# Loading and splitting three weight matrices on GpSimd inside the last four batches of cross attention

## The reference

```python
# x: 32 x 100 x 256, ctx: 32 x 361 x 256; heads 16 of 16
x = x + tanh(g_xattn) * cross_attention(layernorm(x), ctx, mask)   # 32 batches, Wq, Wk, Wv, Wo: 256 x 256
xn = layernorm(x)
gate_v, gate_o = top2_gates(sigmoid(xn @ sel_v.T)), top2_gates(sigmoid(xn @ sel_o.T))  # sel: 64 x 256 each
q, k = xn @ q_w.T, xn @ k_w.T             # q_w, k_w: 1024 x 256, 8 heads of 128
v = sum_e gate_v[e] * (xn @ v_w[e])       # 8 experts a head
ctx = softmax(q @ k.T * SCALE) @ v
x = x + tanh(g_ffn) * sum_e gate_o[e] * (ctx @ o_w[e])
```

## Time and profile before

| | us |
|---|---|
| median of 3 runs | 1932.93 |
| lowest and highest run | 1931.02, 1933.18 |
| span of the profiled execution | 1928.9 |
| PE busy in it | 1873.3 (97%) |
| DVE, ACT, POOL busy in it | 1496.2, 1135.1, 935.0 |

### The profile page before, as it was taken

How to read it: one execution, slowest core, us unless ns; L and a number is a source line. 1 busy time by engine, 2 the same in 40 slices (tenths; PEclk the granted TensorE clock), 3 DMA queues, 4 the chain that set the end, 5 groups by cost and what they waited for, 6 DMA issues and landing times. The chain is left out here.

```text
span 1928.9 us, 57544 instructions
## 1 busy us (share of the span) xinstructions
PE 1873.3 (97%) x13454; PEld 1146.6 (59%) x13454; DVE 1496.2 (78%) x4309; ACT 1135.1 (59%) x3591; POOL 935.0 (48%) x1368
## 2 busy tenths in 40 slices
PE   6899999999997999999999999999999999999998
PEld 3688888888875555444444445545555555555543
DVE  6788888888887962555555556658999999999989
ACT  3688888888885444444444445445555555555543
POOL 4022222222212012666666666666677676776767
PEclk9999999999998999999999999999999999999999
DMA  6678887888752484000000022122222222222201
GB/s 156 127 116 119 118 120 118 120 120 118 119 87 93 205 330 181 27 27 27 14 27 27 27 85 94 52 64 71 71 80 67 79 75 71 79 69 77 75 13 66
DMA packets 192148, 174.22 MB, mean 90 GB/s; under 512 B 51921, under 2 KB 183378, under 8 KB 190034
## 3 DMA queue, kind: packets, MB, share of 16 engines
q1 hardware_dynamic: 189906, 165.06, 37.9%
q0 software_dynamic: 2176, 8.39, 1.3%
HBM read 112.41 MB, written 60.98 MB: 90 GB/s over the span
## 5 line engine op out<-in xcount | busy, mean ns | idle before, releaser
L1489 POOL TENSOR_TENSOR o_side<-o_side,o_tmp 128x256 f32 (+1 forms) x528 | 396.2, 750 | 196.6 <-POOL o_side L1489 70.5
L1258 PE MATMUL e_pv<-e_vw,e_xhi 128*128 (+1 forms) x1600 | 475.9, 379 | 1.2 <-ACT e_out L1181 1.2
L1191 ACT ACTIVATE big<-e_pv,gates 128x128 f32<-128x128 f32 x800 | 228.6, 369 | 280.1 <-PE e_pv L1258 278.5
L654 ACT ACTIVATE c_ex<-c_sm,c_nmax 100x361 f32<-100x361 f32 x512 | 302.7, 593 | 58.0 <-DVE c_nmax L537 49.5
L1617 ACT ACTIVATE o_tmp<-o_py,gates 128x256 f32<-128x256 f32 x528 | 222.3, 475 | 194.1 <-PE o_py L1689 123.3
L1689 PE MATMUL o_py<-o_whi,a_chi 128*128 128x512 f16 x800 | 304.9, 381 | 0.1
L1689 PE MATMUL o_py<-o_wlo,a_chi 128*128 128x512 f16 x800 | 304.5, 381 | 0.0
L1689 PE MATMUL o_py<-o_whi,a_clo 128*128 128x512 f16 x800 | 304.3, 380 | 0.0
L1258 PE MATMUL e_pv<-e_vw,e_xlo 128*128 (+1 forms) x800 | 303.2, 379 | 0.0
L537 DVE CUSTOM_DVE_ANT_0 c_sm<-c_ps,c_mbias 100x361 f32<-100x361 f32 x512 | 269.0, 527 | 38.4 <-PE c_ps L739 32.6
L1124 DVE TENSOR_SCALAR e_acc<-e_pv,gates 128x128 f32<-128x128 f32 x400 | 121.8, 346 | 225.9 <-PE e_pv L1258 225.8
(11 more groups left out here) (164 smaller groups left out, 3213.4 us busy)
## 6 DMA issues: line engine op xcount, KB each, us to landing
qk<-e_out SPq DMA_DIRECT2D x16, 1600.0 KB, 5.2
c_kst<-k_parts SPq DMA_DIRECT2D x256, 90.2 KB, 4.9
a_q<-qk SPq DMA_DIRECT2D x64, 200.0 KB, 2.4
a_k<-qk SPq DMA_DIRECT2D x64, 200.0 KB, 2.4
v<-e_out SPq DMA_DIRECT2D x20, 640.0 KB, 3.3
a_v<-v SPq DMA_DIRECT2D x64, 200.0 KB
c_ctx<-in_ctx_t SPq DMA_DIRECT2D x32, 361.0 KB, 3.5
e_wst<-in_v_w POOLq DMA_DIRECT2D x8, 1024.0 KB, 7.6
```

The source lines that it names most:

```text
L654: act.activation(ex[:, h % 4, 0:SK], sm[:, h % 4, :], ACT.Exp, scale=-1.0, bias=nmax[:, h % 4:h % 4 + 1], accum_out=den[:, b.par, HEAD[h]: ...
L1191: act.activation(tmp[:, hh, e, :], p_v[:, hh, 1, e * PD:(e + 1) * PD], ACT.Copy, scale=gate).then_inc(s_av, 1)
L1258: last = pe.matmul(p_v[:, hh, half, :], a[:, c, bass.ds(t * P, P)], vw[:, bass.ds(col + (w * DC + c) * VW, 512)], start=j == 0, stop=j == ...
L1489: pool.tensor_tensor(side[:, x.t, :], side[:, x.t, :], tmp[:, slot(x, r), j, :], ALU.add).then_inc(s_pool, 1)
```

## The change

The buffers of the three matrices (e_wst, e_qkhi, e_qklo, e_sst, e_shi, e_slo) are allocated before the first block, beside cross attention's own. SP starts the three loads at the end of its `body(28)`. POOL waits for all three at the end of its own `body(28)`, splits the selector there, and then two of the eight parts of the query and key weights (a part is 128 x 2 x 256 elements) at the end of each of `body(28)` to `body(31)`. In the second block the loads, ACT's and DVE's copies for the three matrices and the waits for them are gone; PE waits for the ninth low part instead, and projects queries and keys in one loop.

```diff
+            def load_router():
+                sp.dma_start(f.sst[:, :, :], sel_t.rearrange("(c p) e -> p c e", p=P)).then_inc(f.s_loaded, 16)
+                for w, src in enumerate((q_t, k_t)):
+                    sp.dma_start(f.wst[:, w, :, :], src.rearrange("(c p) n -> p c n", p=P)
+                                 ).then_inc(f.s_loaded, 16)
+
+            def body_and_router(b):
+                body(b)
+                if isinstance(b.n, int) and b.n == NB - 4:
+                    load_router()
...
-                batches(sp, body)
+                batches(sp, body_and_router)
...
+            def split_selector():
+                pool.wait_ge(f.s_loaded, 48)
+                pool.tensor_scalar(f.shi[:, :, :], f.sst[:, :, :], WS, None, ALU.mult).then_inc(f.s_high, 1)
+                pool.wait_ge(f.s_high, 1)
+                pool.tensor_scalar(f.sst[:, :, :], f.sst[:, :, :], WS, None, ALU.mult).then_inc(f.s_scaled, 1)
+                pool.wait_ge(f.s_scaled, 1)
+                pool.tensor_tensor(f.slo[:, :, :], f.sst[:, :, :], f.shi[:, :, :],
+                                   ALU.subtract).then_inc(f.s_low, 1)
+
+            def split_router(n):
+
+                w, part = divmod(n, PARTS)
+                src = f.wst[:, w, :, part * PART:(part + 1) * PART]
+                cut = slice(w * H * PD + part * PART, w * H * PD + (part + 1) * PART)
+                pool.wait_ge(f.s_loaded, 48)
+                pool.tensor_scalar(f.qkhi[:, :, cut], src, WS, None, ALU.mult).then_inc(f.s_high, 1)
+                pool.wait_ge(f.s_high, n + 2)
+                pool.tensor_scalar(src, src, WS, None, ALU.mult).then_inc(f.s_scaled, 1)
+                pool.wait_ge(f.s_scaled, n + 2)
+                pool.tensor_tensor(f.qklo[:, :, cut], src, f.qkhi[:, :, cut],
+                                   ALU.subtract).then_inc(f.s_low, 1)
+
             def body(b):
                 bias_x(b)
                 if later(b, 1):
                     widen_mask(later(b, 1))
                 if later(b, 3):
                     split(later(b, 3))
+                if isinstance(b.n, int) and b.n >= NB - 4:
+                    if isinstance(b.n, int) and b.n == NB - 4:
+                        split_selector()
+                    for n in range(2):
+                        split_router(2 * (b.n - NB + 4) + n)
...
-            sp.dma_start(sst[:, :, :], sel_t.rearrange("(c p) e -> p c e", p=P)).then_inc(s_sel, 16)
             sp.dma_start(rsb[:, :], rs.partition_broadcast(P)).then_inc(s_rs, 16)
-            sp.dma_start(wst[:, 0, :, :], q_t.rearrange("(c p) n -> p c n", p=P)).then_inc(s_wq, 16)
-            sp.dma_start(wst[:, 1, :, :], k_t.rearrange("(c p) n -> p c n", p=P)).then_inc(s_wk, 16)
...
-                if t == 1:
-                    dve.wait_ge(s_whi, 1)
-                    dve.scalar_tensor_tensor(out=slo[:, :, :], in0=sst[:, :, :], scalar=WS,
-                                             in1=shi[:, :, :], op0=ALU.mult,
-                                             op1=ALU.subtract).then_inc(s_wlo, 1)
             x_lo(NB - 2)
             x_lo(NB - 1)
-            for w in range(2):
-                dve.wait_ge(s_whi, 2 + w)
-                dve.scalar_tensor_tensor(
-                    out=qklo[:, :, w * H * PD:(w + 1) * H * PD], in0=wst[:, w, :, :], scalar=WS,
...
-            act.wait_ge(s_sel, 16)
-            act.activation(shi[:, :, :], sst[:, :, :], ACT.Copy, scale=WS).then_inc(s_whi, 1)
...
-                if t >= NB // 2 and t % 2 == 0:
-                    w, part = divmod((t - NB // 2) // 2, PARTS)
-                    act.wait_ge((s_wq, s_wk)[w], 16)
-                    cut = slice(part * H * PD // PARTS, (part + 1) * H * PD // PARTS)
-                    last = act.activation(qkhi[:, :, w * H * PD:(w + 1) * H * PD][:, :, cut],
-                                          wst[:, w, :, cut], ACT.Copy, scale=WS)
...
             pe.wait_ge(s_p, NT)
-            for part in range(2):
-                pe.wait_ge(s_wlo, 2 + part)
-                with pe.Fori(part * H, (part + 1) * H) as u:
+            pe.wait_ge(f.s_low, SPLIT)
+            with pe.Fori(0, 2 * H) as u:
```

More of the change, by code:

```diff
@@ L323, in stage_queries, with stage_cross @@
         return programs
-def stage_cross(nc, k, sems, queries, cross, x, ctx_t, mask, q_parts, k_parts, big, mv, x1):
+def stage_cross(nc, k, sems, queries, cross, f, x, ctx_t, mask, q_parts, k_parts, big, mv, x1, sel_t, q_t, k_t):
     LAG_T, LAG_C, LAG_E, LAG_A = 3, 4, 3, 5
@@ L884, in _, with stage_experts_in @@
             rest()
-def stage_experts_in(nc, k, sems, big, mv, sel_t, q_t, k_t, v_t, rs, qk_out, v_out):
+def stage_experts_in(nc, k, sems, f, big, mv, v_t, rs, qk_out, v_out):
     with ExitStack() as ctx:
@@ L896, in stage_experts_in @@
         pick1 = k.gates[:, :].rearrange("p (g e) -> p g e", e=E)
-        wst = m.sbuf("e_wst", [P, 2, DC, H * PD])
-        qkhi, qklo = (m.sbuf(f"e_qk{n}", [P, DC, 2 * H * PD], F16) for n in ("hi", "lo"))
-        sst = m.sbuf("e_sst", [P, DC, P])
-        shi, slo = (m.sbuf(f"e_s{n}", [P, DC, P], F16) for n in ("hi", "lo"))
+        wst, qkhi, qklo, shi, slo = f.wst, f.qkhi, f.qklo, f.shi, f.slo
         std, rstd, half = (m.sbuf(n, [SQ, NB]) for n in ("e_std", "e_rstd", "e_half"))
@@ L948, in stage_experts_in @@
         QF = 4
-        PARTS = NB // 8
+        SPLIT = 9
         def sync(sp):
@@ L1233, in tensor @@
             pe.wait_ge(s_p, NT)
-            for part in range(2):
-                pe.wait_ge(s_wlo, 2 + part)
-                with pe.Fori(part * H, (part + 1) * H) as u:
-                    for w in range(NC):
-                        pe.wait_ge(s_qe, NC * u + w + 1)
-                        tok = slice(w * NW, (w + 1) * NW)
-                        for n, (c, a, b) in enumerate((c, a, b) for c in range(DC)
-                                                      for a, b in ((qkhi, xhi), (qkhi, xlo), (qklo, xhi))):
-                            last = pe.matmul(p_q[:, w % QF, 0:NW], a[:, c, bass.ds(u * PD, PD)],
-                                             b[:, c, tok], start=n == 0, stop=n == 3 * DC - 1)
-                        last.then_inc(s_qk, 1)
+            pe.wait_ge(f.s_low, SPLIT)
+            with pe.Fori(0, 2 * H) as u:
+                for w in range(NC):
+                    pe.wait_ge(s_qe, NC * u + w + 1)
+                    tok = slice(w * NW, (w + 1) * NW)
+                    for n, (c, a, b) in enumerate((c, a, b) for c in range(DC)
+                                                  for a, b in ((qkhi, xhi), (qkhi, xlo), (qklo, xhi))):
+                        last = pe.matmul(p_q[:, w % QF, 0:NW], a[:, c, bass.ds(u * PD, PD)],
+                                         b[:, c, tok], start=n == 0, stop=n == 3 * DC - 1)
+                    last.then_inc(s_qk, 1)
             pe.wait_ge(s_qe, QF + 2 * H * NC)
@@ L1758, in constants, with router_weights @@
     return k
+def router_weights(nc, ctx, sems):
+    f = Constants()
+    m, held = Store(nc, ctx), Store(nc, sems)
+    f.wst = m.sbuf("e_wst", [P, 2, DC, H * PD])
+    f.qkhi, f.qklo = (m.sbuf(f"e_qk{n}", [P, DC, 2 * H * PD], F16) for n in ("hi", "lo"))
+    f.sst = m.sbuf("e_sst", [P, DC, P])
+    f.shi, f.slo = (m.sbuf(f"e_s{n}", [P, DC, P], F16) for n in ("hi", "lo"))
+    f.s_loaded, f.s_high, f.s_scaled, f.s_low = (held.sem(f"e_s_w{n}") for n in ("load", "high", "scale", "low"))
+    return f
 def cross_inputs(nc, ctx):
@@ L1796, in flamingo @@
             mv = m.sbuf("x1_mv", [P, NB, 2])
-            with ExitStack() as innermost, ExitStack() as sems:
+            f = router_weights(nc, inner, sems)
+            with ExitStack() as innermost, ExitStack() as own:
                 c = cross_inputs(nc, innermost)
-                queries = stage_queries(nc, k, sems, c, big, x, g_xattn, g_ffn, wq, bq, ctx_t, (wk, wv, wo), (bk, bv, bo), q_parts)
-                cross = stage_cross(nc, k, sems, queries, c, x, ctx_t, mask, q_parts, k_parts, big, mv, x1)
+                queries = stage_queries(nc, k, own, c, big, x, g_xattn, g_ffn, wq, bq, ctx_t, (wk, wv, wo), (bk, bv, bo), q_parts)
+                cross = stage_cross(nc, k, own, queries, c, f, x, ctx_t, mask, q_parts, k_parts, big, mv, x1, sel, qw, kw)
                 stage_attention_in(nc, queries, cross)
-            e = stage_experts_in(nc, k, sems, big, mv, sel, qw, kw, vw, rs, qk, v)
+            e = stage_experts_in(nc, k, sems, f, big, mv, vw, rs, qk, v)
         o = stage_attention_out(nc, k, sems, e, x1, qk, v, ow, y)
```

16 lines of the change are left out of this document (7 added, 9 removed).

## The result

| | before | after |
|---|---|---|
| median (runs), us | 1931.97 (4) | 1953.59 (4) |
| lowest and highest run | 1928.89, 1933.18 | 1953.23, 1954.52 |
| profiled execution: own time, span | not listed, 1928.9 | 1953.69, 1951.9 |
| PE, DVE, ACT, POOL busy | 1873.3, 1496.2, 1135.1, 935.0 | 1879.8, 1496.1, 1133.2, 968.1 |

The changed kernel is slower by 21.6 us: ratio 1.0116, interval 1.0104 to 1.0128. 1945.0 was forecast, and 1953.6 lies outside the range, on the expected side. Only 1.8 us lie between the span and the time of one execution here, not 4.0: with as much around it, the profiled execution of before took 1930.7 us, 2.2 under the median of three on which the forecast stood, and 1.3 under that of the four here.

A forecast was written before the change was run, and what follows sets the result against it. PE, busy for 97% of the span, was taken as the bound. Stall +13.8, clock +1.0, POOL against DVE +1.2 and second block -3.9 gave +12.1 us on 1932.9: 1945.0, range 1938.4 to 1952.

The forecast's parts named there:

- The landing: Cross attention: all three late loads have landed at 554.9 us, bounds 551.3 and 557.4.
- POOL's work: Before batch 30: selector 2.5 us, two parts 8.55, batch 29's x bias 0.74, batch 30's mask 0.50.
- The stall: Cross attention: DVE begins batch 30's head 0 at 567.4 instead of 553.63, +13.8 us, bounds +9.8 and +16.4.
- Clock, and POOL against DVE: Batches 30, 31 and block end: PE at half clock after the pause, +1.0 us; three DVE copies meeting POOL, +1.2.
- The second block: PE's shorter wait, kept clock, and ACT's and DVE's removed copies gain there: -3.9 us, bounds -1.5 and -5.3.
- The base: Whole kernel before: profiled 1928.9 us plus 4.0 around it, the median of three runs, 1932.9.
- Rival 2: Cross attention: POOL's splits much shorter, the queue holds batch 30; +3.3 us, 1936; chance 0.05.
- Rival 3: Cross attention: queue far worse, weights land only at 560; +17 to +20 us, 1951; chance 0.12.
- rival 4: Stall there, but batches 30 and 31 then run quicker; +8 to +9 us, 1941; chance within the forecast's 0.80.

The follow-up runs named there:

- e4: Changed kernel with the three loads moved to the beginning of cross attention, POOL's work left in place; 1937.24 us, ratio 1.0021.
- e6: Changed kernel with its late loads kept, but POOL splits only behind batch 30's mask; 1948.47 us, ratio 1.0078.
- e1: Changed kernel with the projection of queries and keys put back into two loops; 1951.59 us, ratio 1.0094.
- e7: Changed kernel with a 128 x 1 memset on POOL at the start of every middle tile of the last stage; 1953.62 us, ratio 1.0108.
- e9: Changed kernel with loads at cross attention's beginning and a 128 x 1 POOL memset at each last-stage middle tile; 1938.83 us, ratio 1.0024.
- e16: Changed kernel with loads at the beginning of cross attention and all splitting in batches 0 and 1; 1956.44 us, ratio 1.0115.
- e18: Changed kernel with early loads, splitting in batches 0 and 1 and also ahead of POOL's wait for the output bias; 1940.17 us, ratio 1.0043.
- e2: Kernel before with the projection as one loop of 16 turns, waiting for both low parts; 1935.35 us, ratio 1.0017.
- e3: Kernel before with only the six buffers given the changed kernel's placement; 1932.19 us, ratio 0.9991.
- e8: Kernel before with a 128 x 64 DVE memset before every last-stage low part from the second head on; 1932.37 us, ratio 0.9995.
- e14: Kernel before with a 128 x 128 ACT copy ahead of each high part of the output weights, heads 1 to 7; 1944.64 us, ratio 1.0056.
- e10: Kernel before with a 128 x 256 DVE memset ahead of each low part of the output weights, heads 1 to 7; 1933.58 us, ratio 1.0004.

## Why the prediction was wrong, point by point

- **The landing** (554.9). It was 559.8. Of these 4.9 us, 3.1 are the lateness of the whole run at batch 29's mask, 1.3 SP's later issues (550.08 where 3.1 more than 545.7 would be 548.8; the store ahead of the three loads is as late, so it isn't of their making), 0.5 the flight of 9.7 us instead of the 7.7 + 1.5 forecast. This term was 1.8 too small.
- **POOL's work** (2.5 + 8.55 + .74 + .50). Measured from 559.88 to 572.22: 12.34 us, against 12.29. Right. The stall was so 15.7 us against 13.8 (572.44 less 553.63 less 3.1), within its bounds.
- **Clock, and POOL against DVE** (+1.0, +1.2). From batch 30's head 0 to the second block: 39.53 us against 38.56, +1.0 for both. The clock was 0.81 in the 14.6 us behind the pause, 0.19 under the full one, some 2.8 us of work (an estimate); the wait for batch 31's mask, 1.10 us before, was gone, and part of the rest was won back too, as the term had it. The copies c_rdx of batches 29 to 31 took 0.53, 0.29 and 0.29 us. The first began 0.39 us ahead of the end of one of POOL's operations and ended 0.14 behind it, which is what the exclusive lock gives; the second ran from 591.97 to 592.26 inside an operation of POOL's (591.21 to 592.73) and was not held, which the lock does not give; the third came when POOL was done. By the sum this term was too large by 1.2. It was luck of the meeting more than a wrong price: in e4 the same three copies took 0.44, 1.04 and 0.56 us.
- **The second block** (-3.9). It was -4.1, by the way that was forecast: PE waits 0.66 us for the last sigmoid and starts the projection 24.9 us into the block instead of 27.6 (2.7 us, against 1.5 + 0.8 + 0.3), and the first steps come 0.17 us apart (1.3). The bound of -5.3 is more than the terms' own upper ends add to, 5.0; nothing hangs on it.
- **The base** (1928.9 + 4.0). Of the 4.0, 1.8 lie around the instructions and 2.2 are luck of the one profiled execution. It cost the forecast nothing, since the base was the median anyway.
- **What failed** is the sum's silence on the last stage. I looked for operations that share ports with POOL only where POOL got new work, and put down nothing for places where the change adds none. There the kernel held, without anybody's intention, a tie within 0.03 us between DVE and POOL, won by DVE. With the change DVE pauses 0.1 us longer ahead of its low part and loses it, and that stands behind the 7.3 us (6.6 of them turn by turn) that make up most of the miss of 8.6. Up to the second block the forecast missed only by 0.7 (1.9 too little in the stall, 1.2 too much in the contention); the second block gave back 0.2 more; the 0.8 left is scatter of the runs.
- **The rivals.** Rival 2's mechanism is real (e6: 6.9 us from the queue alone), but POOL's chain of 12 us lay over it. Rival 3, with 1951 for a landing at 560, came near in time and not in cause: the landing was at 559.8, but 3.1 us of that are the lateness of the whole execution. Of rival 4 one part showed, the vanished wait for batch 31's mask; the clock outweighed it, and the two batches were not quicker.

What stays open: why DVE pauses there. The tie is lost in each of the eight profiles with the new second block and no effective edit at the tie (after, e1, e4, e6, e7, e9, e16, e18), and won in each of the four with the old one (before, e2, e3, e8), so it isn't chance from run to run; neither PE's loop alone nor the placement alone does it, and PE's loop put back doesn't undo it. The pause tells the kernels apart without exception: 0.14 us between the two register instructions in heads 1, 3 and 5 (0.39 once, at the first part of head 1) in all fourteen profiles with the new second block, 0.04 in all six with the old one. What these fourteen share on that engine is a DVE list that has three instructions fewer ahead of the last stage (4306 on the page of the changed kernel's profile, 4309 before). A pause of the same 0.1 us stands elsewhere in the old kernels, ahead of the `o_main` that DVE makes 4.6 us ahead of the low part in heads 2, 4 and 6, where DVE has time; it stays when PE's, ACT's or the buffers' side is changed (e2, e3, e14) and goes when a memset is added to DVE's loop (e8, e10) and with the new second block. So the pauses seem to hang on where DVE's instructions lie in its list. That is inferred: no run changed DVE's list alone in the second block, and ACT's is shorter too in all fourteen.

## What to carry to other kernels

Work that is moved into an engine's idle time is late by what it waits for, and everything queued behind it on that engine is as late: ask for the landing of its data and for the next instruction behind it, not for the busy share. A load of megabytes put into the queue of small periodic loads delays these too, even where nobody waits for the load itself (6.9 us in e6). And when a change moves the time in a stage that it doesn't touch, compare the longest and the median duration of each operation in the loop there: where two engines meet at one port within hundredths of a microsecond, an edit elsewhere can decide who is first (here DVE's list, three instructions shorter, went with 0.1 us), and a loop repeats the decision. Look at what each of the two did just ahead of the meeting, its register instructions too.

## What the runs showed of the hardware that was not expected

- A DVE operation with two SBUF inputs and a POOL addition that meet within 0.03 us are not slowed both by a little: one keeps 0.69 or 0.73 us, the other takes 1.19 or 1.25. In one order it cost the kernel nothing, in the other 0.5 us a turn (with DVE's pause, 0.6).
- The one that waits ends its own length less 0.15 us behind the end of the other: 0.54 for 0.69 (after), 0.59 for 0.73 (before), 0.14 for the 0.29 of a copy c_rdx (after, 575.36 to 575.50).
- In one profile the tie fell the same way in nearly every turn (11 of 11 in the changed kernel, 10 of 11 in e1), and kernels that differ only in another stage fell differently. Head 7, 0.01 us apart, was won by DVE in both kernels.
- DVE's list has pauses of 0.1 us between two register instructions that wait for nothing the trace shows, at the same place in each turn. They are at other places in a kernel whose DVE list has three instructions fewer ahead of the loop.
- An instruction of 0.1 us in front of another one can cost nothing: in e8 the gap of 0.2 us between a released wait and DVE's instruction took the memset whole.
